# Attention stage of a four-layer graph network: one DMA transpose for each half and unit, the exponent's bias from one SBUF input, the diagonal on GpSimd

## The chip, the cores and the metric

One NeuronCore of one Trainium2 chip. The metric is device time in microseconds (us) of one execution; lower is better. The engines are TensorE (PE, matmuls; its weight loads are PEld), VectorE (DVE), ScalarE (ACT), GpSimd (POOL) and SyncE (SP), which here only issues DMAs. Each engine runs its own list of instructions in order and waits on semaphores.

## What is computed

Four layers over a graph of 2708 nodes with 512 features; the change is in layer 0. Its core, cut from the reference:

```python
adj = jnp.maximum(adjacency_matrix, jnp.eye(n))
keys = jnp.einsum('nj,hjk->hnk', node_matrix, Wks)
queries = jnp.einsum('nj,hjk->hnk', node_matrix, Wqs)
values = jnp.einsum('nj,hjk->hnk', node_matrix, Wvs)
atts = jnp.einsum('hqk,hmk->hqm', queries, keys) / key_dim ** 0.5
atts = atts - 1e+16 * (1.0 - adj)[None, :, :]
atts = jax.nn.softmax(atts, axis=-1)
return jnp.einsum('hqm,hmk,hko->qo', atts, values, Wo)
# then x = layernorm(x + this); 8 heads of 64
```

Layer 1 and layer 3 multiply the adjacency with x and a weight matrix, layer 2 is an attention with one head over all 512 features (the edge stage).

## The kernel before, in words

The nodes are padded to 22 tiles of 128 rows (T = 22). Keys and values of all nodes lie in SBUF as float16 pairs, a high half and the low rest, so that products come out nearly in float32. The function attention works through 176 units: one unit is one query tile and one head h, and i = 8 t + h is its number. Every engine runs its own step for each h of each tile, and works in it on units of different age (`back` in `unit` is how many units back):

- PE (L696): scores of unit i in three pieces (L659) into two PSUM slots; turn of unit i - 2 (L670), the PE transposes of the last 10 of 22 key blocks in three groups; the far products of unit i - 3 (L684, L679), 12 key blocks whose probabilities were transposed by DMA; scores of the third piece; the near products of unit i - 3. At h = 5 of the next tile PE transposes the tile's result o (L704), at h = 6 it multiplies with Wo (L708, helper L98).
- DVE (L828): the mask (L797) adds the adjacency bias to the scores, writes them to SBUF and keeps the largest of each row; largest (L807) joins the three maxima to the negative bias of the exponent; near_rest (L823) makes the low halves of the turned blocks; diagonal (L816) at h = 6 sets the diagonal block of the next tile's bias to 0; at h = 6 also the residual and the statistics of the norm.
- ACT (L755): the exponent (L742) of unit i - 1 in three pieces, the high halves of the turned blocks (L751), the high half of columns 1024 to 1535 (L781), the copy of the products out of PSUM (L763).
- POOL (L621): the high half of columns 0 to 1023 (L629), then at some h a piece of the next tile's adjacency bias (L612), the normalised result (L636) or the norm (L421, L424, L433), then the two low halves (L618) of unit i - 1.
- SP (L579): for unit i - 1 four DMA transposes (L589), high half columns 0 to 1023, high 1024 to 1535, low 0 to 1023, low 1024 to 1535; each waits until PE has used that buffer (far_used) and until its part is made (part_high, part_low). Then the loads of the step (L560): a piece of the next tile's adjacency at h 0 to 3, of its queries at h 4 and 5, a store at h 6, a row block of x at h 7.

The buffers of a unit are doubled by v, the parity of h. POOL's and ACT's copies into part wait for the landing of the transposes of two units before (far_ready), DVE's mask for POOL's subtraction of two units before (part_low). The first three tiles are written out; tiles 3 to 20 run in a loop whose body is two tiles (nine rounds); the last follows it. FAR is the pair of column ranges of the DMA transposes, ADJ_PARTS the four pieces of the adjacency row. The edge stage uses the same kind of transposes (L990), two of 8 blocks of 128 columns and one of 6 for each half and tile.

Of the kernel before, what the change touches and what calls it, by code (L numbers as in the profile page):

```python
# [459 lines left out]
def attention(nc, layer, x_rows, out_rows, q_rows, adj_rows, kk, vv, wo, ident):  # L460
# [5 lines left out]
    with ExitStack() as ctx:  # L466
# [13 lines left out]
        mx, nmax = s.sb("mx", [P, 2, NC]), s.sb("nmax", [P, 2])  # L480
        ln_p, lifted = s.sb("ln_p", [P, NC]), s.sb("lifted", [P, NC])
# [8 lines left out]
        pad_clear, ones_ready, ln_p_ready = s.sem("pad_clear"), s.sem("ones_ready"), s.sem("ln_p_ready")  # L490
        off_diag_scaled = s.sem("off_diag_scaled")
# [8 lines left out]
        far_ready = [[s.sem(f"far_ready{c}{v}") for v in range(2)] for c in range(len(FAR))]  # L500
        far_used = [s.sem(f"far_used{c}") for c in range(len(FAR))]
# [47 lines left out]
        def _(sp):  # L549
# [29 lines left out]
            def step(m, u, h, on):  # L579
                if on(1):  # L580
                    i, _t, _u, h1, same = unit(m, u, h, 1)
                    v = h1 % 2
                    for a, made in enumerate((part_high, part_low)):
                        for c, (lo, width) in enumerate(FAR):
                            k = slice(lo // P, (lo + width) // P)
                            if not early(i, 2):
                                wait_apart(sp, far_used[c], i - 1, pad_clear)
                            wait_apart(sp, made[c], i + 1, pad_clear)
                            sp.dma_start_transpose(far[a][:, v, k, :], part[a][:, v, lo:lo + width]) \  # L589
                                .then_inc(far_ready[c][v], 16)  # L590
                loads(m, u, h)
# [9 lines left out]
        def _(pool):  # L601
            nc.gpsimd.memset(adj[:, :, N:NP], -BIG).then_inc(pad_clear, 1)
            nc.gpsimd.memset(vv[:, :, :, P:P + 1], 1.0).then_inc(ones_ready, 1)
            nc.gpsimd.memset(ln_p[:, :], -LN_P).then_inc(ln_p_ready, 1)
            norm.exponent(nc, pool)
            nc.gpsimd.tensor_scalar(out=off_diag[:, :], in0=ident[:, :], scalar1=BIG, scalar2=-BIG, op0=ALU.mult,
                                    op1=ALU.add).then_inc(off_diag_scaled, 1)

            def bias(m, u, n):
# [3 lines left out]
                                        scalar2=-BIG, op0=ALU.mult, op1=ALU.add).then_inc(bias_ready, 1)  # L613

# [6 lines left out]
            def step(m, u, h, on):  # L621
                if on(1):
# [3 lines left out]
                    if not early(i, 2):  # L626
                        wait_apart(pool, far_ready[0][v], 32 * same, pad_clear)
# [13 lines left out]
                if on(1):  # L641
                    low(i, v, 0)
                    low(i, v, 1)

            for n in range(len(ADJ_PARTS)):
                bias(0, 0, n)
            all_steps(pool, step)

        @block.tensor
        def _(pe):  # L650
# [33 lines left out]
            def far_products(i, v, h, same, c):  # L684
                lo, width = FAR[c]
                if c == 0 and not early(i, 1):
                    pe.wait_ge(pv_out, i)
                pe.wait_ge(far_ready[c][v], 32 * same + 32)
                products(v, h, range(lo // P, (lo + width) // P)).then_inc(far_used[c], 1)
# [6 lines left out]
            def step(m, u, h, on):  # L696
# [21 lines left out]
                if on(3):  # L718
                    k, _t, _u, h3, same = unit(m, u, h, 3)
                    far_products(k, h3 % 2, h3, same, 0)  # L720
                    far_products(k, h3 % 2, h3, same, 1)
# [15 lines left out]
        def _(act):  # L737
            def exp(i, v, c):
                lo, width = PIECES[c]
                if c == 0:  # L740
                    act.wait_ge(nmax_ready, i + 1)
                nc.scalar.activation(sc[:, v, lo:lo + width], sc[:, v, lo:lo + width], ACT.Exp,  # L742
                                     bias=nmax[:, v:v + 1]).then_inc(exp_done, 1)
# [11 lines left out]
            def step(m, u, h, on):  # L755
# [20 lines left out]
                if on(1):  # L776
                    lo, width = FAR[1]
                    if not early(i, 2):
                        act.wait_ge(far_ready[1][v], 32 * same)
# [8 lines left out]
        def _(dve):  # L788
            def mask(i, u, h, c):
                v, (lo, width) = h % 2, PIECES[c]  # L790
                if not early(i, 2):
# [7 lines left out]
                    in1=adj[:, u, lo:lo + width], scale=1.0 / (Q_S * Q_S), scalar=-3.0e38,  # L799
                    op0=ALU.add, op1=ALU.max, accum_out=mx[:, v, c:c + 1]).then_inc(slot_free, 1)  # L800

            def largest(i, v):

                if not early(i, 2):
                    dve.wait_ge(exp_done, NC * (i - 1))
                wait_apart(dve, slot_free, NC * (i + 1), pad_clear)
                nc.vector.tensor_tensor_reduce(out=lifted[:, :], in0=mx[:, v, :], in1=ln_p[:, :], scale=-1.0,  # L807
                                               scalar=3.0e38, op0=ALU.add, op1=ALU.min,
# [706 lines left out]
```

## Time and profile before

| | |
|---|---|
| median of 3 runs | 2759.59 us (2759.41 to 2773.42) |
| the profiled execution | 2765.6 us, span from first to last instruction 2763.7 us |
| mean granted TensorE clock | 0.972 |
| PE / DVE / ACT / POOL busy | 2536.4 / 1690.2 / 1360.0 / 1127.7 us |
| attention stage | about 213 to 1440 us of the span |
| DMA transposes in the stage | 352 high and 352 low |

Busy time is the time in which an engine has an instruction under way; of PE it is modelled, since matmuls are pipelined. SP's own instructions are those of its queue (SPq): for a DMA the time of the issue, not of the transfer; the view of a tile gives the time from issue to landing apart. A wait is put down to the instruction that ended it.

### The profile page before, as it was taken

How to read it: one execution, taken by the hardware profiler on the slowest of the kernel's cores; microseconds unless marked ns; L12 is line 12 of the kernel's file. 1: busy time of each engine (PE TensorE's matmuls, PEld its weight loads, DVE VectorE, ACT ScalarE, POOL GpSimd, SP SyncE). 2: the span in 40 equal slices, each digit the busy share in tenths (PEclk: the TensorE clock that was granted, in tenths of full speed). 3: DMA queues.
4: the chain of work that ended last, by engine and by line, in shares of the span. 5: the costliest groups of instructions: out<-in, count | busy, mean ns of one | idle time of the engine just before them, and what ended most of it. 6: DMA issues, size and time to landing. Idle time of an engine off the chain costs nothing. (4 is left out here: it accounts for less than half of the span.)

```text
span 2763.7 us, 68614 instructions
## 1 busy us (share of the span) xinstructions
PE 2536.4 (92%) x25068; PEld 1575.8 (57%) x25068; DVE 1690.2 (61%) x3036; ACT 1360.0 (49%) x2024; POOL 1127.7 (41%) x946
## 2 busy tenths in 40 slices
PE   7997998989989999899978999798999999979998
PEld 6875666666666666666654444475444444434443
DVE  3347998889889888898963222355445556633222
ACT  3336777767667767676753222222424333323221
POOL 0006777777767777677750133100111111210222
PEclk9998999999999999999998999899999999989999
DMA  3117999999999999899964455312556667732554
GB/s 126 61 57 147 166 165 157 157 164 159 156 159 164 157 161 157 159 166 153 162 107 140 148 202 199 137 46 71 153 156 162 177 176 205 190 124 82 199 206 147
DMA packets 789165, 412.94 MB, mean 149 GB/s; under 512 B 701920, under 2 KB 723168, under 8 KB 780512
## 3 DMA queue, kind: packets, MB, share of 16 engines
q1 hardware_dynamic: 788960, 409.86, 66.2%
q8 instruction: 171, 2.80, 0.4%
q14 instruction: 34, 0.28, 0.0%
HBM read 201.15 MB, written 38.44 MB: 87 GB/s over the span
## 5 line engine op out<-in xcount | busy, mean ns | idle before, releaser
L742 ACT ACTIVATE att_scores<-att_scores,att_nmax 128x1024 f32<-128x1024 f32 x528 | 551.4, 1045 | 166.0 <-DVE att_nmax L807 164.6
L797 DVE CUSTOM_DVE_ANT_0 att_scores<-att_slots,att_adj 128x1024 f32<-128x1024 f32 x528 | 573.6, 1087 | 36.9 <-PE att_slots L659 30.3
L618 POOL TENSOR_TENSOR att_part_low<-att_scores,att_part_high 128x1024 f16<-128x1024 f32 x352 | 574.5, 1652 | 50.2 <-ACT att_part_high L781 39.7
L659 PE MATMUL att_slots<-l_kk,att_q 128*128 128x512 f16 x2112 | 484.6, 365 | 51.4 <-issue 31.5
L1343 PE MATMUL a_ps<-l_y,a_adj 128*128 128x512 f16 (+1 forms) x1936 | 430.0, 381 | 9.0 <-DVE a_adj L1357 4.7
L823 DVE TENSOR_TENSOR att_near_low<-att_ps_t,att_near_high 128x512 f16<-128x512 f32 x528 | 314.8, 596 | 61.7 <-ACT att_near_high L751 60.4
L751 ACT ACTIVATE att_near_high<-att_ps_t 128x512 f16<-128x512 f32 x528 | 256.0, 520 | 179.2 <-PE att_ps_t L670 177.7
L1343 PEld LDWEIGHTS a_ps<-l_y,a_adj 128*128 128x128 f16 (+1 forms) x1936 | 182.7, 98 | 256.4 <-issue 40.5
L659 PEld LDWEIGHTS att_slots<-l_kk,att_q 128*128 128x128 f16 x2112 | 195.2, 100 | 230.6 <-issue 54.4
L1088 PE MATMUL edge_ps_o<-l_sup,edge_pt_high 128*128 128x512 f16 x968 | 288.0, 379 | 0.0
L679 PE MATMUL att_ps_pv<-l_vv,att_far_high 128*128 128x65 f16 (+1 forms) x4224 | 219.0, 193 | 64.6 <-DMA att_far_low<-att_part_low 64.4
L670 PE MATMUL att_ps_t<-all_ident,att_scores 128*128 128x128 f32 x1760 | 260.1, 279 | 9.2 <-DVE att_near_low L823 6.2
L629 POOL CAST att_part_high<-att_scores 128x1024 f16<-128x1024 f32 x176 | 182.6, 1037 | 194.3 <-ACT att_scores L742 135.4
L1327 ACT ACTIVATE a_adj<-l_adj 128x2816 f16<-128x2816 f32 x44 | 112.0, 2549 | 298.2 <-DMA l_adj<-in_adj_cols 278.0
L679 PEld LDWEIGHTS att_ps_pv<-l_vv,att_far_high 128*128 128x128 f16 x4224 | 207.1, 98 | 83.5 <-DMA att_far_low<-att_part_low 45.8
L1074 PE MATMUL edge_slots<-l_ht 128*128 128x512 f16 x1104 | 203.3, 344 | 16.1 <-DVE edge_mx L1182 14.4
L679 PE MATMUL att_ps_pv<-l_vv,att_far_low 128*128 128x65 f16 x2112 | 212.8, 195 | 0.0
L670 PEld LDWEIGHTS att_ps_t<-all_ident,att_scores 128*128 128x128 f32 x1760 | 189.0, 138 | 39.4 <-issue 8.6
L679 PEld LDWEIGHTS att_ps_pv<-l_vv,att_near_high 128*128 128x128 f16 x3520 | 183.8, 97 | 43.7 <-issue 2.3
L679 PE MATMUL att_ps_pv<-l_vv,att_near_high 128*128 128x65 f16 x3520 | 203.1, 193 | 0.0
L1029 POOL TENSOR_TENSOR edge_xb<-edge_xres,all_b_row 128x512 f32<-128x512 f32 x22 | 28.3, 1287 | 414.6 <-DVE edge_residual L1226 406.1
L679 PE MATMUL att_ps_pv<-l_vv,att_near_low 128*128 128x65 f16 x1760 | 196.5, 194 | 0.0
(150 smaller groups left out, 4013.4 us busy)
## 6 DMA issues: line engine op xcount, KB each, us to landing
l_adj<-in_adj_cols SPq DMA_DIRECT2D x44, 1408.0 KB, 6.0
l_adj_tiles<-in_adj SPq DMA_DIRECT2D x22, 1354.0 KB, 6.0
att_adj<-in_adj SPq DMA_DIRECT2D x66, 384.0 KB, 3.6
p_x_in<-x SPq DMA_DIRECT2D x66, 256.0 KB, 2.6
att_q<-q_rows SPq DMA_DIRECT2D x44, 256.0 KB, 3.6
a_xres<-x SPq DMA_DIRECT2D x44, 256.0 KB, 2.8
scores_rows<-edge_raw SPq DMA_DIRECT2D x8, 842.0 KB, 3.4
p_x_in<-in_x SPq DMA_DIRECT2D x22, 256.0 KB, 2.7
```

Source lines behind the costliest of these rows:

```text
L618: nc.gpsimd.tensor_tensor(out=part[1][:, v, lo:lo + width], in0=sc[:, v, lo:lo + width], in1=part[0][:, v, lo:lo + width], op=ALU.subtract ...
L629: nc.gpsimd.tensor_copy(part[0][:, v, lo:lo + width], sc[:, v, lo:lo + width]) \
L659: mm = nc.tensor.matmul(slots[:, slot, z:z + w], q[:, u, h % 2, a, h // 2, :], kk[:, h, lo + z:lo + z + w], start=a == 0, stop=a == 1)
L670: mm = nc.tensor.transpose(ps_t[0:r, g, n * P:(n + 1) * P], sc[:, v, k * P:k * P + r], ident[:, :])
L679: mm = nc.tensor.matmul(ps_pv[:, 0:cols.stop - cols.start], halves[a][0:r, v, n, :], vv[0:r, k, h, cols], start=k == 0 and a + b == 0, sto ...
L742: nc.scalar.activation(sc[:, v, lo:lo + width], sc[:, v, lo:lo + width], ACT.Exp, bias=nmax[:, v:v + 1]).then_inc(exp_done, 1)
L751: nc.scalar.activation(near[0][:, v, n:n + len(tiles), :], ps_t[:, g, 0:w].rearrange("p (k r) -> p k r", r=P), ACT.Copy) \
L797: nc.vector.tensor_tensor_reduce(out=sc[:, v, lo:lo + width], in0=slots[:, (NC * h + c) % 2, 0:width], in1=adj[:, u, lo:lo + width], scale ...
L823: nc.vector.tensor_tensor(out=near[1][:, v, n:n + len(tiles), :], in0=ps_t[:, g, 0:w].rearrange("p (k r) -> p k r", r=P), in1=near[0][:, v ...
L1074: mm = nc.tensor.matmul(slots[:, slot, z:z + w], ht[a][:, j, bass.ds(t * P, P)], ht[b][:, j, lo + z:lo + z + w], start=k == 0, stop=k == l ...
L1088: mm = nc.tensor.matmul(ps_o[:, u, :], pt[a][0:r, k, :], sup[b][0:r, k, :], start=k == 0 and a + b == 0, stop=k == T - 1 and a == 1)
L1343: mm = nc.tensor.matmul(ps[:, u, :], a16[0:r, u, k, :], y[b][0:r, k, :], start=k == 0 and b == 0, stop=k == T - 1 and b == 1)
```

## The change

Three edits in attention. First, SP issues one DMA transpose of all 12 blocks for the high half and one for the low half. The semaphores far_ready and far_used have no column range any more, so the high transpose waits for both part_high, the low one for both part_low; PE's far products of a unit are one group with one wait; POOL's and ACT's copies wait until both transposes of two units before have landed. Second, the mask writes negated scores and keeps the smallest of them, the exponent has scale=-1.0, and the bias of the exponent is made by a tensor_scalar with one SBUF input and constants in place of an operation on two SBUF inputs. Third, the diagonal block is multiplied with 1 - identity (0 on the diagonal) by POOL at the end of h = 5, where DVE took a maximum with a table at h = 6.

```diff
--- before.py
+++ after.py
@@ -477,8 +477,7 @@
         rinv = s.sb("rinv", [P, H, 1])
         o = s.sb("o", [P, D])
         ot = s.sb("ot", [P, 2, J, P], F16)
-        mx, nmax = s.sb("mx", [P, 2, NC]), s.sb("nmax", [P, 2])
-        ln_p, lifted = s.sb("ln_p", [P, NC]), s.sb("lifted", [P, NC])
+        least, nmax, lifted = s.sb("least", [P, 2, NC]), s.sb("nmax", [P, 2]), s.sb("lifted", [P, NC])
         norm = Norm(s, outs=1)
         slots = s.ps("slots", [P, 2, CHUNK])
         ps_t = s.ps("ps_t", [P, NT, BANK])
@@ -487,8 +486,8 @@
         adj_loaded = [[s.sem(f"adj_loaded{n}{u}") for u in range(2)] for n in range(len(ADJ_PARTS))]
         q_loaded = [s.sem(f"q_loaded{u}") for u in range(2)]
         xres_loaded = s.sem("xres_loaded")
-        pad_clear, ones_ready, ln_p_ready = s.sem("pad_clear"), s.sem("ones_ready"), s.sem("ln_p_ready")
-        off_diag_scaled = s.sem("off_diag_scaled")
+        pad_clear, ones_ready = s.sem("pad_clear"), s.sem("ones_ready")
+        off_diag_ready = s.sem("off_diag_ready")
         bias_ready = s.sem("bias_ready")
         diag_ready = s.sem("diag_ready")
         slot_full = s.sem("slot_full")
@@ -497,8 +496,8 @@
         exp_done = s.sem("exp_done")
         part_high = [s.sem(f"part_high{c}") for c in range(len(FAR))]
         part_low = [s.sem(f"part_low{c}") for c in range(len(FAR))]
-        far_ready = [[s.sem(f"far_ready{c}{v}") for v in range(2)] for c in range(len(FAR))]
-        far_used = [s.sem(f"far_used{c}") for c in range(len(FAR))]
+        far_ready = [s.sem(f"far_ready{v}") for v in range(2)]
+        far_used = s.sem("far_used")
         rest_clear = s.sem("rest_clear")
         turned = s.sem("turned")
         near_high = [s.sem(f"near_high{g}") for g in range(NT)]
@@ -580,14 +579,12 @@
                 if on(1):
                     i, _t, _u, h1, same = unit(m, u, h, 1)
                     v = h1 % 2
+                    if not early(i, 2):
+                        wait_apart(sp, far_used, i - 1, pad_clear)
                     for a, made in enumerate((part_high, part_low)):
-                        for c, (lo, width) in enumerate(FAR):
-                            k = slice(lo // P, (lo + width) // P)
-                            if not early(i, 2):
-                                wait_apart(sp, far_used[c], i - 1, pad_clear)
+                        for c in range(len(FAR)):
                             wait_apart(sp, made[c], i + 1, pad_clear)
-                            sp.dma_start_transpose(far[a][:, v, k, :], part[a][:, v, lo:lo + width]) \
-                                .then_inc(far_ready[c][v], 16)
+                        sp.dma_start_transpose(far[a][:, v, :, :], part[a][:, v, :]).then_inc(far_ready[v], 16)
                 loads(m, u, h)
 
             for half in range(2):
@@ -601,16 +598,23 @@
         def _(pool):
             nc.gpsimd.memset(adj[:, :, N:NP], -BIG).then_inc(pad_clear, 1)
             nc.gpsimd.memset(vv[:, :, :, P:P + 1], 1.0).then_inc(ones_ready, 1)
-            nc.gpsimd.memset(ln_p[:, :], -LN_P).then_inc(ln_p_ready, 1)
             norm.exponent(nc, pool)
-            nc.gpsimd.tensor_scalar(out=off_diag[:, :], in0=ident[:, :], scalar1=BIG, scalar2=-BIG, op0=ALU.mult,
-                                    op1=ALU.add).then_inc(off_diag_scaled, 1)
+            nc.gpsimd.tensor_scalar(out=off_diag[:, :], in0=ident[:, :], scalar1=-1.0, scalar2=1.0, op0=ALU.mult,
+                                    op1=ALU.add).then_inc(off_diag_ready, 1)
 
             def bias(m, u, n):
                 lo, width = ADJ_PARTS[n]
                 wait_apart(pool, adj_loaded[n][u], 16 * m + 16, pad_clear)
                 nc.gpsimd.tensor_scalar(out=adj[:, u, lo:lo + width], in0=adj[:, u, lo:lo + width], scalar1=BIG,
                                         scalar2=-BIG, op0=ALU.mult, op1=ALU.add).then_inc(bias_ready, 1)
+
+            def diagonal(m, u):
+
+                t = 2 * m + u
+                wait_apart(pool, bias_ready, len(ADJ_PARTS) * (t + 1), pad_clear)
+                part_of = adj[:, u, bass.ds(t * P, P)]
+                nc.gpsimd.tensor_tensor(out=part_of, in0=part_of, in1=off_diag[:, :], op=ALU.mult) \
+                    .then_inc(diag_ready, 1)
 
             def low(i, v, c):
                 lo, width = FAR[c]
@@ -624,7 +628,7 @@
                     v = h1 % 2
                     lo, width = FAR[0]
                     if not early(i, 2):
-                        wait_apart(pool, far_ready[0][v], 32 * same, pad_clear)
+                        wait_apart(pool, far_ready[v], 32 * same, pad_clear)
                     wait_apart(pool, exp_done, NC * i + 1, pad_clear)
                     nc.gpsimd.tensor_copy(part[0][:, v, lo:lo + width], sc[:, v, lo:lo + width]) \
                         .then_inc(part_high[0], 1)
@@ -641,9 +645,13 @@
                 if on(1):
                     low(i, v, 0)
                     low(i, v, 1)
+                if h == BIAS_STEPS[-1] and not is_tile(m, u, T - 1) and not is_tile(m, u, T):
+                    diagonal(*after(m, u))
 
             for n in range(len(ADJ_PARTS)):
                 bias(0, 0, n)
+            pool.wait_ge(off_diag_ready, 1)
+            diagonal(0, 0)
             all_steps(pool, step)
 
         @block.tensor
@@ -681,12 +689,11 @@
                                               stop=k == T - 1 and a == 1)
                 return mm
 
-            def far_products(i, v, h, same, c):
-                lo, width = FAR[c]
-                if c == 0 and not early(i, 1):
+            def far_products(i, v, h, same):
+                if not early(i, 1):
                     pe.wait_ge(pv_out, i)
-                pe.wait_ge(far_ready[c][v], 32 * same + 32)
-                products(v, h, range(lo // P, (lo + width) // P)).then_inc(far_used[c], 1)
+                pe.wait_ge(far_ready[v], 32 * same + 32)
+                products(v, h, range(TK)).then_inc(far_used, 1)
 
             def near_products(i, v, h):
                 for g in range(NT):
@@ -717,8 +724,7 @@
                     turn(j, h2 % 2, 0)
                 if on(3):
                     k, _t, _u, h3, same = unit(m, u, h, 3)
-                    far_products(k, h3 % 2, h3, same, 0)
-                    far_products(k, h3 % 2, h3, same, 1)
+                    far_products(k, h3 % 2, h3, same)
                 if on(2):
                     turn(j, h2 % 2, 1)
                     if h in (5, 6) and not is_tile(m, u, 0):
@@ -740,7 +746,7 @@
                 if c == 0:
                     act.wait_ge(nmax_ready, i + 1)
                 nc.scalar.activation(sc[:, v, lo:lo + width], sc[:, v, lo:lo + width], ACT.Exp,
-                                     bias=nmax[:, v:v + 1]).then_inc(exp_done, 1)
+                                     bias=nmax[:, v:v + 1], scale=-1.0).then_inc(exp_done, 1)
 
             def near_halves(i, v, g):
                 tiles = TURN_GROUPS[g]
@@ -776,7 +782,7 @@
                 if on(1):
                     lo, width = FAR[1]
                     if not early(i, 2):
-                        act.wait_ge(far_ready[1][v], 32 * same)
+                        act.wait_ge(far_ready[v], 32 * same)
                     act.wait_ge(exp_done, NC * i + 2)
                     nc.scalar.activation(part[0][:, v, lo:lo + width], sc[:, v, lo:lo + width], ACT.Copy) \
                         .then_inc(part_high[1], 1)
@@ -796,25 +802,18 @@
                 wait_apart(dve, slot_full, NC * i + c + 1, pad_clear)
                 nc.vector.tensor_tensor_reduce(
                     out=sc[:, v, lo:lo + width], in0=slots[:, (NC * h + c) % 2, 0:width],
-                    in1=adj[:, u, lo:lo + width], scale=1.0 / (Q_S * Q_S), scalar=-3.0e38,
-                    op0=ALU.add, op1=ALU.max, accum_out=mx[:, v, c:c + 1]).then_inc(slot_free, 1)
+                    in1=adj[:, u, lo:lo + width], scale=-1.0 / (Q_S * Q_S), scalar=3.0e38,
+                    op0=ALU.add, op1=ALU.min, accum_out=least[:, v, c:c + 1]).then_inc(slot_free, 1)
 
             def largest(i, v):
+
 
                 if not early(i, 2):
                     dve.wait_ge(exp_done, NC * (i - 1))
                 wait_apart(dve, slot_free, NC * (i + 1), pad_clear)
-                nc.vector.tensor_tensor_reduce(out=lifted[:, :], in0=mx[:, v, :], in1=ln_p[:, :], scale=-1.0,
-                                               scalar=3.0e38, op0=ALU.add, op1=ALU.min,
-                                               accum_out=nmax[:, v:v + 1]).then_inc(nmax_ready, 1)
-
-            def diagonal(m, u):
-
-                t = 2 * m + u
-                dve.wait_ge(bias_ready, len(ADJ_PARTS) * (t + 1))
-                part_of = adj[:, u, bass.ds(t * P, P)]
-                nc.vector.tensor_tensor(out=part_of, in0=part_of, in1=off_diag[:, :], op=ALU.max) \
-                    .then_inc(diag_ready, 1)
+                nc.vector.tensor_scalar(out=lifted[:, :], in0=least[:, v, :], scalar1=LN_P, scalar2=3.0e38,
+                                        op0=ALU.add, op1=ALU.min, accum_out=nmax[:, v:v + 1]) \
+                    .then_inc(nmax_ready, 1)
 
             def near_rest(i, v, g):
                 tiles = TURN_GROUPS[g]
@@ -859,8 +858,6 @@
                     near_rest(j, h2 % 2, 2)
                 if on(0):
                     mask(i, u, h, 2)
-                if h == 6 and not is_tile(m, u, T - 1) and not is_tile(m, u, T):
-                    diagonal(*after(m, u))
                 if on(0):
                     largest(i, h % 2)
                 if on(2):
@@ -869,9 +866,6 @@
             rest = len(TURN_GROUPS[-1]) * P
             nc.vector.memset(ps_t[:, NT - 1, rest - P:rest], 0.0).then_inc(rest_clear, 1)
             dve.wait_ge(pad_clear, 1)
-            dve.wait_ge(ln_p_ready, 1)
-            dve.wait_ge(off_diag_scaled, 1)
-            diagonal(0, 0)
             all_steps(dve, step)
```

## Rows read from the trace of the kernel before

**Rows 1.** The page, span in 40 slices: DMA busy share.
```profile
DMA  3117999999999999899964455312556667732554
```
**Rows 2.** Windows, the stage: length, busy PE, PEld, DVE, ACT, POOL, clock, DMA share, GB/s.
```profile
213.20:1420.00 1206.80, 1095.98 (x15582) 797.71 (x15583) 1058.02 (x2050) 869.59 (x1413) 892.12 (x696) 0.97 0.92 158
```
**Rows 3.** Windows of single units: h2, h4, h6, h7; h0, h3, h5, h7; h0.
```profile
721.27:726.90 5.63, 5.63 (x92) 4.38 (x89) 5.46 (x12) 4.91 (x9) 4.29 (x5) 1.00 1.01 216
...
732.59:738.76 6.17, 6.17 (x95) 4.82 (x93) 6.03 (x13) 5.11 (x9) 5.96 (x5) 1.00 0.94 155
...
747.33:752.94 5.61, 5.61 (x89) 4.36 (x88) 5.07 (x10) 3.10 (x6) 4.13 (x5) 1.00 0.75 160
752.94:759.65 6.71, 5.95 (x91) 4.23 (x89) 6.71 (x13) 4.42 (x9) 5.22 (x4) 1.00 1.04 141
...
1203.30:1209.10 5.80, 5.80 (x92) 4.21 (x89) 5.66 (x12) 4.81 (x10) 4.31 (x4) 1.00 0.96 160
...
1222.68:1232.03 9.35, 7.58 (x91) 5.34 (x89) 6.73 (x14) 5.56 (x9) 7.42 (x7) 0.82 0.86 168
...
1238.14:1246.35 8.21, 8.21 (x102) 5.54 (x100) 6.73 (x15) 6.94 (x12) 6.95 (x7) 1.00 0.87 143
...
1251.96:1262.29 10.33, 6.04 (x92) 4.35 (x89) 9.28 (x17) 6.72 (x11) 7.50 (x6) 1.00 1.02 161
...
706.90:715.65 8.75, 8.39 (x89) 5.67 (x89) 4.03 (x7) 3.11 (x6) 3.30 (x3) 0.66 0.94 124
```
**Rows 4.** Timeline of SP's queue: start, length, line, DMA, count merged.
```profile
609.90 2.60 SPq L589 DMA_TRANSPOSE att_far_high<-att_part_high  x2
612.66 2.59 SPq L589 DMA_TRANSPOSE att_far_low<-att_part_low  x2
615.46 0.42 SPq L557 DMA_DIRECT2D att_adj<-in_adj  x1
616.11 2.71 SPq L589 DMA_TRANSPOSE att_far_high<-att_part_high  x2
618.98 2.59 SPq L589 DMA_TRANSPOSE att_far_low<-att_part_low  x2
```
**Rows 5.** Waits of SP's queue, 240 to 1420 us, all: total us, times, longest.
```profile
SPq L58 <- ACT att_part_high L781: 3.4, 4, 1.0
SPq L58 <- PE att_ps_pv L679: 1.3, 3, 1.0
SPq L58 <- POOL att_part_low L618: 0.4, 1, 0.4
```
**Rows 6.** Timeline of SP's queue, single issues: 8 blocks, 4 blocks, 6 blocks (edge).
```profile
612.66 1.24 SPq L589 DMA_TRANSPOSE att_far_low<-att_part_low  x1
...
614.06 1.19 SPq L589 DMA_TRANSPOSE att_far_low<-att_part_low  x1
...
2188.76 1.21 SPq L990 DMA_TRANSPOSE edge_pt_high<-edge_part_high  x1
```
**Rows 7.** Views of att_far_low and edge_pt_high: issue ns and landing us, least/median/most.
```profile
L589 SPq DMA_TRANSPOSE att_far_low<-att_part_low x352: 1188/1231/2489, 229.0 to 1432.1; - x176
...
DMA to landing us min/median/max: 2.4/3.3/5.8
...
DMA to landing us min/median/max: 2.7/3.2/3.3
```
**Rows 8.** Timelines of POOL and of SP's queue, same unit.
```profile
647.51 3.25 POOL L618 TENSOR_TENSOR att_part_low<-att_scores,att_part_high 128x1024 f16<-128x1024 f32 x2
...
653.45 2.59 SPq L589 DMA_TRANSPOSE att_far_low<-att_part_low  x2
```
**Rows 9.** Waits of PE, 240 to 1420 us: total us, times, longest.
```profile
PE att_ps_pv L679 <- DMA att_far_low<-att_part_low: 61.8, 68, 2.3
PE att_slots L659 <- issue: 31.5, 14, 4.0
```
**Rows 10.** Views of DVE's lines 807 and 816: ns least/median/most.
```profile
L807 DVE CUSTOM_DVE_ANT_0 att_lifted<-att_mx,att_ln_p x176: 148/950/2010, 223.7 to 1421.8; 128x3 f32<-128x3 f32 x176
...
L816 DVE TENSOR_TENSOR att_adj<-att_adj,att_off_diag x22: 291/1506/1782, 218.9 to 1363.1; 128x128 f32 x18, 128x128 f32<-128x128 f32 x4
```
**Rows 11.** View of att_pv: POOL's line 636, ns least/median/most.
```profile
L636 POOL TENSOR_TENSOR att_o<-att_pv,att_rinv x22: 1042/1045/1048, 294.5 to 1437.7; 128x512 f32<-128x512 f32 x22
```

## Prediction

> **What bounds the kernel now.** The change touches the attention stage alone, so I first cut that stage out with the view of windows: from the first score product to the last units it takes 1206.8 us for 176 units (22 tiles of 8 heads), 6.86 us a unit, and TensorE (PE) is busy for 1096.0 us of it [rows 2]. That is 91%, which looks like PE; DVE has 1058. The page's slices say that the DMA engines are busy too [rows 1]. A share does not tell what ends last, so I went on to single units [rows 3]. In a unit of the plain kind PE is busy from end to end in 5.61 to 5.63 us. That is PE's own pace, and every unit above it was held by something. Head 4 (with four transposes of o before the next unit) takes about 6.1, head 5 (with the output product before the next) 8.21. The slow ones are h0 at 5.80, h7 at 6.71, an h3 of 9.35 (granted clock 0.82), and at the turn of the loop over tile pairs 10.33 and then 8.75 at clock 0.66.
>
> What holds them is on the issuing queue. In the timeline of SyncE's queue (SP) the four transposes of a unit come in pairs of 2.6 us, an adjacency load stands between, and the next high pair starts at once: 609.90, 616.11, 622.4 [rows 4]. The waits of this queue over 1180 us of the stage add up to 5.1 us in three rows [rows 5]. A queue that never waits and always issues is the bound. The data are ready long before: the two low subtractions of one unit end at 650.76, and the low pair is issued at 653.45 [rows 8]. So the transposed halves come late, and PE waits for them 68 times, 61.8 us in all [rows 9]; after such waits come stretches at the lower of the clock's two levels (1.2 instead of 2.4 GHz), as in the h3 of 9.35, which PE pays a second time.
>
> Behind it is DVE. In the h0 of 5.80 it is busy 5.66 [rows 3]. L807, a reduction of three numbers, takes 950 ns at the median and 148 at the least, and L816 (128x128) 1506 against 291 [rows 10].
>
> **Part 1: two transposes in place of four.** The issue of a transpose costs nearly the same whatever it moves: 1.24 us for 8 blocks of 128 columns, 1.19 for 4, 1.21 for the 6 blocks of the edge stage [rows 6]. That is 0.011 us a block, so 12 blocks should cost 1.28 us. The long tail to 2.5 us [rows 7] is not a matter of size, and I let it stand for each issue. SP has now 4 issues of 1.24 to 1.4 a unit plus gaps of 0.17 to 0.2 and loads of 0.4 to 0.7; after, 2 of 1.3 to 1.5 and the same loads, about 3.9 us. Bounds: 1.2 us (the 6- and 4-block rows) and 2.6 us (the pair as it stands, nothing but a gap saved). I take 1.28, as three sizes lie on one line.
>
> The waits that it adds: the high transpose waits for ACT's half too, the low one for both subtractions, and behind the waiting instruction on SP stand only the next low pair and loads. Landing takes 2.7 us for 6 blocks and 3.2 for 8 in the quiet edge stage, which gives 4.0 for 12; the attention stage goes up to 5.8 [rows 7]. At 5.6 us a unit the low issue comes some 6.7 us after PE has started the scores of the step in which the exponent is taken, it lands at 10.7 to 12.5, and PE wants it two steps later, at 2 x 5.6 + 2.1 = 13.3. The one tight place is h6, where GpSimd (POOL) does the norm's 2.8 us before the subtractions; there it lands at about 13 and PE may wait 0 to 1 us once a tile. POOL's copy into the buffer now waits for both whole landings, also at 13.3: the same margin. The single wait of PE for both halves costs nothing where both have landed.
>
> **Part 2: the bias of the exponent.** L807 has two SBUF inputs now and will have one. Its times run from 148 to 2010 ns for the same three numbers, so it waits inside for something; POOL's subtraction (up to 2152 ns) ran beside it each time that I looked. The cover is DVE's slack, which is nil at h0 and h7. I take 0.15 to 0.2 us after, from the least of [rows 10]; the other end is today's 0.95. The Trainium skill (SBUF — State Buffer, Who interferes with whom) says that a Vector instruction with two SBUF inputs contends with a GpSimd one that reads SBUF, and that tensor_scalar in the form that writes its accumulator does not take the pair; the spread of L807 agrees with the first half, no row here shows the second. The sign turned in the mask and in the exponent changes no operand's size: nothing, and if it were 1% of 3.3 us a unit on DVE, 0.03 us under PE's pace.
>
> **Part 3: the diagonal on POOL.** DVE loses 22 times 1.5 us between the last mask of h6 and L807, so in the very step that makes h7 cost 6.71. POOL gets 22 times 0.3 us: 512 columns with two inputs take 1045 ns [rows 11], a quarter is 0.26; at worst 1.5. It runs at the end of h5, behind the subtractions that others wait for, and its user starts three units later. It delays h6's copy by 0.3 us at most. DVE saves 0.8 + 1.5 us in h6, more than the 1.1 by which h7 exceeds PE's pace, so h7 should fall to 5.6 to 5.8.
>
> **The sum.** With SP, L807 and the diagonal out of the way PE's pace remains: 6 x 5.62 + 6.1 + 8.2 = 48.0 us a tile, 1056 for 22. The turns of the loop stay, since there PE waits for nothing that the trace shows (31.5 us of "issue" [rows 9]) while SP goes on: 8 turns x (10.33 - 6.71 + 8.75 - 5.80) = 52 us. Together 1108, so 99 us less than 1206.8. From that I take off 20 us, 0.11 a unit, for what is still uneven (the tight h6, DVE at 5.2 to 5.4 a unit under 5.62, landings that meet a load), and add 2 for the last unit's shorter backlog: 81 us. The profiled execution took 2765.6 us (span 2763.7), so 2685 for one like it; the median of the runs is 2759.59, and I state the prediction against that: 2679 us. Without the 20 it would be 2659.
>
> **Rivals.**
> 1. The reduction stays slow (0.95 us, by whatever it waits for). Then DVE leads at 5.80, and h7 keeps about half its excess: (6 x 0.18 + 0.6 + 0.3) x 22 = 44 us come back: 2722. For it: DVE is next in line in every h0. Against: 148 ns occurs with the same sizes. Chance 0.11.
> 2. The issue costs by what it moves, so a merged one takes what its two did less the gap. SP keeps leading and saves 2 x 0.17 us a unit, 60 us at most, and the longer landing takes some of it: 2700 to 2750, I say 2725. A DMA page of the Trainium skill (DMA: Bandwidth & Descriptors, Why a DMA increments its semaphore by 16 and not by 1) gives, for generations before the newest, 262,144 sequencer cycles for a transpose within SBUF of 8,192 tiles, a cost for each tile; by that rule this rival would be the forecast. The rows of three sizes speak against it (2 more blocks add 0.02 us). Chance 0.08.
> 3. Slower: the longer landing closes a ring. POOL's copy waits for the landing of two units before; copy, two subtractions, issue and landing must fit in two units. They take 4.5 us plus L. For L under 6.7 the ring is slack; it costs against today from 2 x 6.86 - 4.5 = 9.2 us on. If 12 blocks landed after 10 us, a unit would take 7.25 and the kernel 2760 + 0.39 x 176 = 2830. Against: 5.8 is the longest of all landings, with four transposes queued. Chance 0.03.
> 4. SP is no bound but only looks full, and something that I take for free (loads that come in bunches, DMA engines near their share) holds the unit above 6.7: 2735 to 2765. For it: the share is 0.92 [rows 2]. Against: single units of 5.61 show shares from 0.75. Chance 0.05.
>
> **Chances.** The forecast, 2655 to 2705, has 0.73. The range 2652 to 2728 takes in rivals 1 and most of 2. Some 0.5% is what a measurement of this kernel can tell from no change: faster by more 0.93, within it 0.04 (part of 4), slower 0.03 (3).
>
> **What would show it.** Two transposes a unit at 1.28 us each and a queue of SP with long waits for POOL's subtractions; PE's waits for the far halves under 15 us; L807 under 0.2 us; L816 gone from DVE; units of 5.6 us at h0 to h3 and h7; loop turns unchanged; granted clock in the stage above 0.97. The forecast is wrong if the merged issue takes over 2 us, if landings go beyond 7, or if DVE is busy through a whole unit.

## Result and the profile after

The changed kernel takes 2665.57 us (median of 4 runs, 2663.17 to 2668.39) against 2766.03 us for the kernel before, run again beside it (4 runs); the ratio of the two is 0.9633 with a 95% interval of 0.9612 to 0.9653. That is 100 us less. The forecast was 81 us less, from a median of 2759.59 us for the kernel before.

The windows of the stage and of single units (length, then busy PE, PEld, DVE, ACT, POOL, granted clock, DMA share, GB/s) answer to [rows 2] and [rows 3]:

```profile
212.70:1325.00 1112.30, 1072.48 (x15606) 805.97 (x15606) 920.21 (x2031) 875.11 (x1415) 900.07 (x718) 0.97 0.94 172
614.78:620.40 5.62, 5.62 (x91) 4.37 (x89) 5.08 (x12) 4.91 (x9) 4.33 (x4) 1.00 1.34 216
...
651.57:660.98 9.41, 5.67 (x91) 4.35 (x89) 6.17 (x16) 6.94 (x11) 8.72 (x7) 1.00 0.82 140
660.98:670.42 9.44, 8.60 (x88) 6.02 (x88) 4.02 (x7) 3.10 (x6) 1.79 (x2) 0.64 0.53 90
...
603.56:609.16 5.60, 5.60 (x91) 4.35 (x89) 4.85 (x12) 5.01 (x9) 5.45 (x4) 1.00 0.63 120
```

The stage is shorter by 94 us between about the same first and last units. A plain unit takes 5.62 us with PE busy throughout, h7 takes 5.60 (it was 6.71), and the slow h2 and h3 are gone. Only the turn of the loop is left: an h7 of 9.41 and the h0 behind it of 9.44 at a granted clock of 0.64.

The waits of SP's queue over 240 to 1320 us (total us, times, longest) answer to [rows 5]:

```profile
SPq L58 <- ACT att_part_high L787: 149.6, 127, 4.2
SPq L58 <- PE att_ps_pv L687: 57.2, 26, 5.2
SPq L58 <- POOL att_part_low L622: 44.2, 61, 1.7
```

and those of PE in the same stretch to [rows 9]:

```profile
PE att_slots L667 <- issue: 34.7, 16, 3.9
PE att_ps_pv L687 <- DMA att_far_low<-att_part_low: 0.2, 1, 0.2
```

The queue that waited for 5 us in all now waits for over 250: it has time to spare. Most of it is waiting for ACT's part of the high half, not for POOL's subtractions as the prediction had named. PE's 61.8 us of waiting for the far halves have shrunk to 0.2. The view of the new line of the transposes answers to [rows 7] (ns least/median/most, then the landing in us):

```profile
L587 SPq DMA_TRANSPOSE att_far_high<-att_part_high x176: 1279/1534/2672, 225.0 to 1329.7; - x176
L587 SPq DMA_TRANSPOSE att_far_low<-att_part_low x176: 1414/1617/3357, 228.1 to 1331.7; - x176
...
DMA to landing us min/median/max: 3.6/4.2/6.3
```

The view of the new reduction on DVE answers to [rows 10]:

```profile
L814 DVE TENSOR_SCALAR_CACHE_REDUCE att_lifted<-att_least x176: 155/156/159, 222.1 to 1325.2; 128x3 f32<-128x3 f32 x176
```

and the view of the diagonal, now on POOL, to [rows 10, 11]:

```profile
L616 POOL TENSOR_TENSOR att_adj<-att_adj,att_off_diag x22: 450/457/466, 217.1 to 1264.9; 128x128 f32 x18, 128x128 f32<-128x128 f32 x4
```

### The profile page after: what moved, and what is told of

The parts are those of the page before. It is cut to its first block and busy times, and to the rows that moved or that the text cites. A ratio compares the mean times of both kernels' runs of the same rounds, so it can differ in the third digit from the quotient of the medians.

```text
span 2664.4 us, 67769 instructions
## 1 busy us (share of the span) xinstructions
PE 2511.2 (94%) x25068; PEld 1583.2 (59%) x25068; DVE 1549.8 (58%) x3014; ACT 1364.3 (51%) x2024; POOL 1134.1 (43%) x967
## 5 line engine op out<-in xcount | busy, mean ns | idle before, releaser
L667 PE MATMUL att_slots<-l_kk,att_q 128*128 128x512 f16 x2112 | 478.2, 363 | 48.8 <-issue 34.7
L687 PEld LDWEIGHTS att_ps_pv<-l_vv,att_far_high 128*128 128x128 f16 x4224 | 215.3, 98 | 5.8 <-issue 3.5
L687 PEld LDWEIGHTS att_ps_pv<-l_vv,att_far_low 128*128 128x128 f16 x2112 | 196.1, 98 | 0.0
```

What stands on the lines that cost most here:

```text
L667: mm = nc.tensor.matmul(slots[:, slot, z:z + w], q[:, u, h % 2, a, h // 2, :], kk[:, h, lo + z:lo + z + w], start=a == 0, stop=a == 1)
L687: mm = nc.tensor.matmul(ps_pv[:, 0:cols.stop - cols.start], halves[a][0:r, v, n, :], vv[0:r, k, h, cols], start=k == 0 and a + b == 0, sto ...
```

## Experiments

The theory is that of the prediction: before the change SP's queue sets the pace, behind it come DVE and then PE. The main rivals are that the two edits on DVE carry part of the gain on their own, and that not the number of issues but the size of the transfers or the joined waits did it. Each ratio is to the kernel before, run beside it; in brackets stands its 95% interval. The kernel before itself came out at 2766 to 2772 us in these comparisons, so times of different experiments compare to about 6 us, and the ratios do better. The length of a unit is taken from the start of its first score product on PE to that of the next.

**The merge alone.** The kernel before with the first of the three edits (its main lines; the semaphores are joined as in the change):

```diff
-    for c, (lo, width) in enumerate(FAR):
-        ...
-        sp.dma_start_transpose(far[a][:, v, k, :], part[a][:, v, lo:lo + width])
+    sp.dma_start_transpose(far[a][:, v, :, :], part[a][:, v, :]).then_inc(far_ready[v], 16)
```

> The kernel before with the merged transposes alone; reduction on two SBUF inputs and diagonal on DVE as before. Theory (the issuing queue was the bound, DVE is next in line): most of the 100 us come, but DVE leads at 5.8 us in the plain units and h7 stays near 6.7: 2700 to 2715 us, ratio to before about 0.98. Rival (the merge gives everything, DVE's two edits nothing): 2666. Rival (the merge gives little without a faster DVE, since both were equally late): above 2735.

Measured: 2695.92 us, ratio 0.9739 (0.9709 to 0.977), so 73 of the 100 us. Windows of an h0 and, from a tile that follows a turn of the loop, of an h1 and an h7:

```profile
513.93:519.73 5.80, 5.80 (x91) 4.21 (x89) 5.66 (x12) 4.81 (x10) 4.32 (x4) 1.00 0.86 119
...
680.46:686.08 5.62, 5.62 (x91) 4.37 (x89) 5.42 (x12) 4.95 (x9) 4.13 (x3) 1.00 0.98 131
717.25:723.96 6.71, 5.96 (x91) 4.34 (x89) 6.71 (x13) 4.41 (x9) 5.22 (x4) 1.00 0.72 151
```

The h0 is at DVE's 5.80 as forecast, with DVE busy 5.66, and h7 stays at 6.71. The time is still 4 us better than the lower end of what was expected (2700). The mechanism is right; the price of what is left on DVE was put too high, for two reasons. The reduction takes 678 ns here at the median, not the 950 of [rows 10]. And within the loop the excess of h0 to h3 stands in every other tile only: in each of the eight tiles behind a turn of the loop h1 to h3 take 5.61 to 5.63 us.

**DVE's two edits alone.** The changed kernel with the four transposes and their semaphores of before.

> The changed kernel with the four transposes of before (with their own semaphores): DVE's two edits alone. Theory: SP's queue still issues without a pause, so the time stays at 2745 to 2766 us (ratio 0.993 to 1.0), and its waits on data stay under 30 us in the stage. Rival (DVE's edits carry half of the gain): 2715.

Measured: 2767.68 us, ratio 1.0003 (0.9987 to 1.002). Waits of SP's queue (all three rows), 240 to 1320 us:

```profile
SPq L58 <- ACT att_part_high L791: 4.7, 4, 1.9
SPq L58 <- PE att_ps_pv L689: 1.1, 1, 1.1
SPq L556 <- DVE att_least L807: 0.5, 1, 0.5
```

The longest wait of PE there:

```profile
PE att_ps_pv L689 <- DMA att_far_low<-att_part_low: 66.2, 69, 2.4
```

DVE is relieved of 134 us (busy 924 us in the windows view of the stage, where [rows 2] had 1058), and the kernel is no faster at all. As long as SP leads, DVE's work is hidden; once it no longer does, the same edits are worth 30 us (2696 to 2666). This is the plainest proof of the order of the three bounds.

**The two edits on DVE apart.** The changed kernel with one of them undone (cut; with the diagonal its table goes back too, with the reduction the constant tile).

```diff
-    nc.gpsimd.tensor_tensor(out=part_of, in0=part_of, in1=off_diag[:, :], op=ALU.mult)
+    nc.vector.tensor_tensor(out=part_of, in0=part_of, in1=off_diag[:, :], op=ALU.max)
```

> The changed kernel with the diagonal back on DVE at h = 6 (maximum with a table on two SBUF inputs). Theory: 1.5 us in the one step where DVE also has residual and statistics; h7 grows from 5.6 to between 5.9 and 6.7, 22 times: 2672 to 2690 us. Rival (DVE's slack of 0.8 us a unit since the cheap reduction hides it): 2666.

```diff
-    nc.vector.tensor_scalar(out=lifted[:, :], in0=least[:, v, :], scalar1=LN_P, scalar2=3.0e38,
+    nc.vector.tensor_tensor_reduce(out=lifted[:, :], in0=least[:, v, :], in1=ln_p[:, :], scale=1.0,
```

> The changed kernel with the reduction on two SBUF inputs again (one of them a constant tile), the diagonal still on POOL. Theory (it waits for POOL's subtraction, 0.8 us a unit): L814 takes 0.15 to 2.0 us, about 0.9 in the mean, DVE leads at 5.8 us in the plain units: 2680 to 2690 us. Rival (the diagonal was what the reduction waited for): 2666.

Measured: 2672.22 us (0.9649, 0.962 to 0.9677) with the diagonal on DVE and 2679.79 us (0.9682, 0.9664 to 0.9701) with the two inputs, against 0.9633 for the changed kernel. Both lie at the lower edge of what was expected. The diagonal is worth some 4 to 7 us, a size at which the intervals of the two ratios overlap; the traces show where it lies, 0.14 us in each h7 and h0 outside the turns. The reduction is worth about 14, and both together 30. h7 is 5.60 us with the reduction undone and 5.74 with the diagonal undone, and 6.71 only with both, since DVE's slack of that step hides nearly all of one but not the two. The h7 with the diagonal on DVE:

```profile
710.45:716.19 5.74, 5.74 (x90) 4.26 (x89) 5.74 (x13) 4.40 (x9) 5.22 (x4) 1.00 0.64 122
```

The reduction's line with the two inputs, and one of its instructions beside POOL's subtraction in the timelines (start, length):

```profile
L816 DVE CUSTOM_DVE_ANT_0 att_lifted<-att_least,att_ln_p x176: 161/674/1179, 224.3 to 1336.3; 128x3 f32<-128x3 f32 x176
...
732.30 1.16 POOL L624 TENSOR_TENSOR att_part_low<-att_scores,att_part_high 128x512 f16<-128x512 f32 x1
732.47 1.00 DVE L816 CUSTOM_DVE_ANT_0 att_lifted<-att_least,att_ln_p 128x3 f32<-128x3 f32 x1
```

The diagonal runs on POOL here, so what the reduction waited for was not the diagonal. Of the 176 reductions 169 take over 0.25 us, and every one of them ends within 0.03 us after a subtraction of POOL has ended. In the kernel before it is 172 of 173. So the reduction is held until POOL's subtraction is through, and its length is what was left of the subtraction when it began. In the changed kernel 175 of the 176 reductions begin under such a subtraction too, and none takes more than 159 ns. What differs is the form of the instruction together with its second SBUF input; no run takes these two apart. So the trace agrees with both halves of the rule of the Trainium skill named in the prediction (SBUF — State Buffer, Who interferes with whom): two inputs are held up beside POOL, the form that writes its accumulator is not.

**Four issues again, with hardly more data.** The changed kernel with two more transposes of one block into a spare tile. PE, ACT and POOL wait for the landing of these too, as they count on the same semaphore.

```diff
     sp.dma_start_transpose(far[a][:, v, :, :], part[a][:, v, :]).then_inc(far_ready[v], 16)
+    sp.dma_start_transpose(spare[:, v, a:a + 1, :], part[a][:, v, 0:P]).then_inc(far_ready[v], 16)
```

> The changed kernel with two more DMA transposes a unit, of one block each into a spare tile: four issues a unit again, with 26 blocks in place of 24. Theory (the number of issues is what counts): SP has 2 x 1.6 + 2 x 1.2 us and loads, near 6.6 us a unit, and the time goes back to 2735 to 2766 us. Rival (the size of the transfers or the joined waits made the gain): 2666 to 2680.

Measured: 2956.51 us, ratio 1.0681 (1.0651 to 1.0712). The direction is the theory's, the size is not: 291 us more than the changed kernel where 70 to 100 were expected. The views of the spare and of the far tile (issue ns least/median/most):

```profile
L589 SPq DMA_TRANSPOSE att_spare<-att_part_high x176: 1221/1528/2827, 226.4 to 1615.9; - x176
...
L588 SPq DMA_TRANSPOSE att_far_high<-att_part_high x176: 1302/1802/2568, 224.9 to 1614.3; - x176
```

SP's waits over 240 to 1500 us:

```profile
SPq L58 <- ACT att_part_high L789: 16.1, 8, 2.6
SPq L58 <- PE att_ps_pv L689: 5.2, 5, 1.6
```

The queue is full again (21 us of waits in 1260), with the same blocks to transpose and the same joined waits as in the changed kernel; so neither the size of the transfers nor the joined waits made the gain. But the number of issues is not the whole price: the kernel before has four issues a unit as well and is 188 us faster. A transpose of one block takes 1.53 us to issue here, more than four blocks in [rows 6]. "A fixed cost and 0.011 us a block" cannot be right behind a large transfer. What sets the pace is the time that the queue's issues take in all.

**Three issues.** The low half in two, the high half in one.

> The changed kernel with the low half transposed in two DMAs (8 and 4 blocks) again: three issues a unit. Theory (SP's queue becomes the bound when its work a unit passes PE's 5.6 to 6.3 us): 1.67 + 2 x 1.3 us, gaps and loads make 5.3 to 5.6 us, just under PE's mean, so 2666 to 2685 us and PE's waits for the far half between 2 and 20 us. Rival (each issue costs in proportion): half way between 2666 and 2766, so 2716.

Measured: 2700.17 us, ratio 0.9756 (0.9739 to 0.9774), between the two expectations. SP's waits, 240 to 1320 us:

```profile
SPq L58 <- ACT att_part_high L792: 30.0, 25, 2.7
SPq L58 <- PE att_ps_pv L692: 22.0, 8, 3.9
SPq L58 <- POOL att_part_low L627: 4.6, 9, 0.6
```

PE's wait for the far half in the same stretch:

```profile
PE att_ps_pv L692 <- DMA att_far_low<-att_part_low: 19.1, 33, 2.1
```

SP is at the edge: 57 us of waits, and PE waits for the far half again in a part of the units. I had counted 1.67 us for the large issue and 1.3 for each small one; they took 1.82 and 1.41 at the median.

**The issue by size.** Transposes of several sizes behind the stage, on quiet engines; then groups without a wait between them. Both kernels ran once, and what counts is read from their traces.

> The changed kernel with transposes of 1, 2, 4, 6, 8, 12 and 24 blocks behind its attention stage, one at a time on quiet engines, twice, and then groups of four issued without a wait between them (12 each; 8 and 4; 12 and 1; 4 each; 1 each). They add work whose result nobody reads. Theory A (a fixed cost and 0.011 us a block): 1.15 us for 1 block, 1.28 for 12, 1.41 for 24, alone and in groups. Theory B (a queue of descriptors that fills): alone as in A, but from the second or third of a group of 12 on 1.5 us and more. Theory C (12 is a dearer number than 4 and 8, whatever the load): 12 alone already 1.43. Landing: 0.2 us a block, so 4.0 for 12 and 6.4 for 24. The time of the kernel grows by about 110 us.

> As the run of sizes, with 8, 10, 12, 14, 16, 18, 20 and 22 blocks alone, twice, and groups of four of 8; of 10; 12 and 8 in turn; of 6. Alone, 8 took 1.23 us, 12 took 1.28 and 1.44, 24 took 3.6. Theory (a queue that holds so many blocks, and beyond them the issue goes at the pace of the transfer, 0.15 us a block): flat to about 12, then a knee, 16 at 1.9 to 2.4, 20 at 2.6 to 3.0. Rival (a step at one number, as between two ways to issue): 14 to 22 all near 3.6. In groups of 8 the issue should stay near 1.3 us if the transfer keeps up (8 x 0.15 = 1.2), in groups of 10 it should rise to 1.5.

Timelines of SP's queue, one issue each. Alone: 1, 8, 12, 24 blocks, and 12 the second time; then the four of 12 in a group; then 12 and the 1 behind it:

```profile
1353.44 1.14 SPq L604 DMA_TRANSPOSE att_far_high<-att_part_high  x1
1363.19 1.23 SPq L604 DMA_TRANSPOSE att_far_high<-att_part_high  x1
1366.25 1.44 SPq L604 DMA_TRANSPOSE att_far_high<-att_part_high  x1
1369.93 3.60 SPq L604 DMA_TRANSPOSE att_far_high<-att_part_high  x1
1388.21 1.27 SPq L604 DMA_TRANSPOSE att_far_high<-att_part_high  x1
...
1397.35 1.44 SPq L610 DMA_TRANSPOSE att_far_high<-att_part_high  x1
1398.83 1.81 SPq L610 DMA_TRANSPOSE att_far_high<-att_part_high  x1
1400.68 1.71 SPq L610 DMA_TRANSPOSE att_far_low<-att_part_low  x1
1402.43 1.95 SPq L610 DMA_TRANSPOSE att_far_low<-att_part_low  x1
...
1413.13 1.43 SPq L610 DMA_TRANSPOSE att_far_high<-att_part_high  x1
1414.61 1.55 SPq L610 DMA_TRANSPOSE att_far_high<-att_part_high  x1
```

The second run of sizes, alone: 14, 16 and 18 blocks.

```profile
1363.36 1.52 SPq L604 DMA_TRANSPOSE att_far_high<-att_part_high  x1
1367.33 1.32 SPq L604 DMA_TRANSPOSE att_far_high<-att_part_high  x1
1371.61 2.71 SPq L604 DMA_TRANSPOSE att_far_high<-att_part_high  x1
```

Alone the issue is nearly flat up to 16 blocks (1.14 to 1.52 us, not quite in order of size: 16 is cheaper than 14, and 12 came at 1.27 once and at 1.43 or 1.44 three times), and then it jumps: 2.71 us for 18, and on to 3.60 for 24. The knee was expected at 12 and soft; it lies between 16 and 18 and is a step. The rival that had 14 to 22 all near 3.6 is out as well.

In groups the issue follows what is still under way. Alone, 24 blocks hold up the next issue, which waits for their landing, 1.77 us longer than 12 do (5.45 us from start to start against 3.68). That is 0.15 us a block, and from it I estimate that a transfer of 12 keeps the DMA engines for 1.8 us and one of 8 for 1.2. In groups of 12 each issue after the first takes 1.71 to 1.95 us; in groups of 10 it takes 1.51 to 1.63, in groups of 8 1.33 to 1.34, of 6 1.29. One block behind 12 takes 1.55 and 1.70 us where it took 1.14 alone. That is what theory B says of groups: an issue is held while the transfers before it are not far enough through. Its other half, "alone as in A", fails beyond 16 blocks, and where in the queue the hold sits no trace shows. It accounts for the dear spare transposes above, and for a merged pair that costs 3.15 us (the two medians) and not 2.6 inside the kernel. Why 12 blocks alone have two prices stays open.

Two smaller expectations missed. The landings come within those 3.68 us for 12 blocks and 5.45 for 24, where 4.0 and 6.4 were expected. And the first run took 2744 us, 79 more than the changed kernel and not 110.

**The loop's turns.** Tiles 3 to 20 written out, in the changed kernel and in the kernel before, and a body of six tiles in place of two.

```diff
-            pairs(eng, 3, T - 1, tile)
+            for t in range(3, T - 1):
+                tile(t // 2, t % 2)
```

> The changed kernel with tiles 3 to 20 of the attention stage written out in place of the loop over pairs. Theory (PE stops at each of 8 turns of the loop and then runs at the lower clock): 8 x 7.3 = 58 us less, 2605 to 2620 us, with h7 at 5.6 and h0 at 5.6 us throughout. Rival (the code that is fetched once for each instruction costs as much, in many short stops): 2650 or more.

> The changed kernel with a loop body of six tiles in place of two: two turns in place of eight. Theory (each turn costs PE 6.4 us, from 51 us for eight): 2614.7 + 2 x 6.4 = 2627 us. Rival (what the written-out code saved was not the turns but something of each tile): between, about 2650.

> The kernel before, with tiles 3 to 20 written out. Theory (SP's queue is the bound and goes on issuing while PE stops at a turn): PE's stops are hidden, 2750 to 2770 us, ratio 0.995 to 1.0. Rival (PE's stops and SP's queue each cost their own time): 2715, as much less as the changed kernel gained.

Measured: 2614.7 us (0.9453, 0.9438 to 0.9469) for the changed kernel written out, 51 us under the changed kernel and the fastest of all. In 900 us of its stage PE stands for 1.2 us, at a granted clock of 1.00:

```profile
300.00:1200.00 900.00, 898.84 (x13490) 684.59 (x13488) 784.02 (x1742) 753.49 (x1220) 773.17 (x617) 1.00 1.01 184
```

The same window of the changed kernel, with 35 us of standing and a clock of 0.97:

```profile
300.00:1200.00 900.00, 865.17 (x12647) 652.73 (x12643) 739.75 (x1633) 704.74 (x1143) 724.60 (x578) 0.97 0.95 172
```

The waits view calls these stops "issue", but the changed kernel's trace has the instruction that they belong to. It is the loop's branch in PE's own queue. The view of the line of the loops' ends (all loops of the kernel, ns least/median/most; PEldq is PE's queue):

```profile
L143 DVEq COMPARE_BRANCH  x73: 50/56/73, 43.0 to 2648.1; - x73
...
L143 PEldq COMPARE_BRANCH  x73: 76/208/4297, 51.7 to 2651.0; - x73
...
L143 SPq COMPARE_BRANCH  x72: 40/45/63, 54.9 to 2642.4; - x72
```

At the eight turns of this stage PE's branch takes 3.74 to 4.30 us, and at the end of the loop, where it falls through, 0.08. In the loop behind the stage, whose rounds last 6 us and not 104, it takes 0.21 to 0.23. DVE, ACT, POOL and SP take 0.04 to 0.07 at the same turns. One turn costs 5.8 to 8.5 us of unit lengths (h7 and the h0 behind it, against 5.60 and 5.62), 7.2 in the mean of the eight: the stop, and then the lower clock.

With six tiles in the body it takes 2635.99 us (0.9512, 0.9484 to 0.954). That is 9 us more than expected as it stands; the kernel before beside it took 6 us more than beside the written-out one, so by the ratios it is 4. By the unit lengths its two turns cost 9.4 and 9.6 us, more than any of the eight. The branch takes 4.2 us in both, hardly more than in the shorter body; the difference is in the h0 behind it, 10.9 and 11.2 us where the eight had 7.8 to 10.3.

The kernel before, written out, takes 2736.13 us (0.9883, 0.9852 to 0.9913), against 2772.4 for the kernel before beside it: 36 us less (27 to 41 by the interval), where at most 14 were expected. That miss does not come from PE. SP's queue waits for 1.0 us in its whole stage, so it leads as before, and its own steps have become shorter. The timeline of its queue, one step:

```profile
622.96 3.16 SPq L590 DMA_TRANSPOSE att_far_low<-att_part_low  x2
626.16 0.64 SPq L553 DMA_DIRECT2D att_q<-q_rows  x1
626.96 2.62 SPq L590 DMA_TRANSPOSE att_far_high<-att_part_high  x2
```

Between low pair and load 0.04 us pass here, where [rows 4] has 0.20 (618.98 + 2.59 to the load at 621.77), and 0.16 from load to high pair against 0.23 (615.88 to 616.11). In the loop the trace has three register instructions of SP in those gaps; written out there is none. 0.23 us a unit over the 144 units of the loop is 33 us, about what was gained. Over the whole stage the gaps between the queue's DMAs add up to 44 us less and its issues to 13 us more, which is the 31 us by which the stage is shorter. That leaves next to nothing for PE's stops at the turns, which were hidden, as the theory says.

## Why the prediction was right, step by step

**The bound.** Right. The merge alone brings 73 us, the other edits alone nothing; four issues bring the full queue back; PE's waits for the far halves went from 61.8 us to 0.2.

**The issue of a merged transpose, 1.28 us.** The step that was mis-sized. 1279 ns is the least of 176, the medians are 1534 and 1617. The line through three sizes holds roughly for one transfer alone and up to 16 blocks; its rows went up to 8, and none showed 12 blocks behind 12. Two issues of 1.6 us leave SP idle enough, so this cost nothing here; that is luck of the margin. With three issues the kernel was 15 to 34 us slower than that price had made me expect, and with four 190 to 220. The upper bound of 2.6 us that I had kept is the rival 2 below: at it most of the gain would have gone.

**Landing, 4.0 us, and the ring.** Right: 4.2 at the median and 6.3 at most, a little over the 5.8 that I had allowed. The wait of 0 to 1 us at h6 that I had feared does not occur: PE waits once in the stage, for 0.2 us, and POOL's copy once, for 0.7.

**The reduction, 0.15 to 0.2 us.** Right (155 to 159 ns). Its rival was priced at 44 us; undoing the reduction costs 14. It then takes 0.67 us at the median and not 0.95, h7 stays at 5.6, and the excess of the other units, 5.73 to 5.79 us in h0 to h3, stands in every other tile of the loop only.

**The diagonal.** POOL takes 457 ns, not 300: the rate of a large operation does not hold for 128 columns. The move brings 4 to 7 us alone, since nearly all of h7's excess goes away when either edit is made.

**The sum.** 48.0 us a tile is what a tile without a turn takes, to the last hundredth of a unit (5.62, 5.62, 5.63, 5.61, 6.11, 8.21, 5.61, 5.60). The turns were priced at 52 us and take 58 by the unit lengths. The error is the 20 us that I took off the gain for unevenness: there is next to none, since every engine but PE has slack in every unit. Without it the forecast was 101 us less, and 100 were measured. The figure named without it, 2659 us, lies 7 us under the measured time all the same; 6 of these are the median that I started from, 2759.59 us, where the kernel before came out at 2766.03 when it was run again. That the gain comes within 1 us of it is in part luck: the stage takes 1112 us and not the 1108 of the sum, but in the profiled executions 5 us are gained outside of the stage and not 2.

**The rivals.** Rival 1 (a slow reduction) did not occur. Rival 2 (issue by size) is refuted as it was put: the pair takes 3.15 us where its four parts took 4.9 (four times the 1.23 of [rows 7]). The cost for each tile that stood beside it, from the Trainium skill (DMA: Bandwidth & Descriptors, Why a DMA increments its semaphore by 16 and not by 1), is at most a small part of the issue up to 16 blocks, 1.14 to 1.52 us in all; beyond 16 the issue does grow with the blocks. Rival 3 needed landings of over 9.2 us and got 6.3. Rival 4 (a full queue that is no bound) is refuted by the two runs with parts of the change.

## What to carry to other kernels

A queue that issues DMAs is an engine like the others: add up its issues, and if it never waits, it is the bound, however idle the transfers look. What the next engine in line is worth can't be read from its busy share; DVE's two edits were worth 0 us before the first bound fell and 30 us after. When all engines but one have slack, look for what that one still stops for: here the turns of a loop, 51 us, gone when the code is written out.

## What was not expected of the hardware

- The issue of a DMA transpose within SBUF is nearly flat from 1 to 16 blocks of 128 x 128 (1.14 to 1.52 us) and steps up to 2.71 us at 18 and 3.60 at 24.
- Behind a transfer of 12 blocks that has just been issued, the next issue takes 1.55 to 1.70 us for 1 block and 1.7 to 1.95 for 12.
- At the turn of a loop with some 1440 matmuls (16 units of 88 and the output products) in its body the branch takes PE 3.7 to 4.3 us, and the other engines under 0.1. The next unit runs in part at the lower clock (granted 0.64 in the one shown). A turn costs 5.8 to 8.5 us; with three times the body 9.4 and 9.6, and the branch in it 4.2.
- A reduction of 128x3 on DVE with two SBUF inputs ends when POOL's subtraction beside it ends and takes up to 2.0 us for it, where it takes 0.15 alone; the tensor_scalar with one input that writes its accumulator takes 0.16 us under the same subtraction.
- Register work between DMAs costs a queue that is the bound: 0.2 us a unit, some 30 us in the kernel before.
